# Bi-directional linear attention of a four-part vision tower: three units on VectorE become six, in two image halves

## The reference, cut to what matters

```python
# L1_attn: bi-directional linear attention over 49 tokens, then channel mixing
def _wkv_scan(w, k, v):
    ...
    def step(carry, kv):
        a, b, m = carry
        kt, vt = kv
        mm = jnp.maximum(m + w, kt)
        e1 = jnp.exp(m + w - mm)
        e2 = jnp.exp(kt - mm)
        return ((e1 * a + e2 * vt, e1 * b + e2, mm), (a, b, m))
    ...
def bi_wkv(w, u, k, v):
    ...
    kk = kt + u
    M = jnp.maximum(jnp.maximum(mf, mb), kk)
    ef = jnp.exp(mf - M)
    eb = jnp.exp(mb - M)
    ec = jnp.exp(kk - M)
    y = (ef * af + eb * ab + ec * vt) / (ef * bf + eb * bb + ec)
    ...
h = _ln(x, ln1_w, ln1_b)
k = h @ Wk_a.T
v = h @ Wv_a.T
sr = jax.nn.sigmoid(h @ Wr_a.T)
y = bi_wkv(decay / Tn, first / Tn, k, v)
x = x + sr * y @ Wo_a.T
h = _ln(x, ln2_w, ln2_b)
kf = jnp.square(jax.nn.relu(h @ Wk_f.T))
x = x + jax.nn.sigmoid(h @ Wr_f.T) * (kf @ Wv_f.T)
```

## Time and profile before

| | us |
|---|---|
| median of 3 runs | 1715.54 (1711.41 to 1716.17) |
| the profiled execution, its own time | 1713.88 |
| its span | 1712.1 |
| PE busy | 1332.6 (78%) |
| DVE busy | 985.0 (58%) |
| ACT busy | 626.3 (37%) |
| POOL busy | 550.1 (32%) |

### The profile page before, as it was taken

One profiled execution on the slowest core, in us unless ns is written; L12 is line 12 of the kernel. 1 busy time (PEld: TensorE's weight loads), 2 busy tenths in 40 slices (PEclk: granted clock), 3 DMA queues, 4 the chain that ended last, 5 costly groups with the idle time before them and its releaser, 6 DMA issues.

```text
span 1712.1 us, 18068 instructions
## 1 busy us (share of the span) xinstructions
PE 1332.6 (78%) x6516; PEld 760.3 (44%) x6516; DVE 985.0 (58%) x1582; ACT 626.3 (37%) x1114; POOL 550.1 (32%) x390
## 2 busy tenths in 40 slices
PE   6789889899898672578687745007978999989998
PEld 6444445445454341343233332003774666744444
DVE  2179999999999998730000067994253661411111
ACT  2577767767677540110000013110404224233111
POOL 0078887888878873000000010000031530100000
PEclk9789999999999987678778757555997999999999
DMA  5213142240321404037878610000012000111100
GB/s 175 85 68 123 39 143 60 92 151 15 139 89 63 150 1 171 1 140 301 336 296 322 249 49 0 0 0 0 1 28 54 1 1 1 33 58 51 33 1 29
DMA packets 41332, 151.95 MB, mean 89 GB/s; under 512 B 10364, under 2 KB 17659, under 8 KB 37020
## 3 DMA queue, kind: packets, MB, share of 16 engines
q1 hardware_dynamic: 37148, 149.21, 24.5%
q10 hardware_dynamic: 4096, 1.58, 0.4%
HBM read 147.56 MB, written 1.63 MB: 87 GB/s over the span
## 4 chain that ended last, share of the span: by engine, by line
PE 48%; DVE 20%; issue 15%; POOL 7%; DMA 6%; ACT 3%; SPq 1%; ACTq 0%; DVEq 0%; POOLq 0%
PE ps L1497 46%; DVE arena L1154 6%; DMA arena<-in_e_b 6%; POOL arena L677 4%; DVE arena L1143 4%; ACT arena L783 1%; DVE arena L1107 1%; DVE stats L1094 1%; POOL arena L698 1%; SPq L535 1%; POOL arena L686 1%; PE ps L1506 1%; POOL arena L682 1%; DVE arena L1380 1%; DMA arena<-in_patches 0%
## 5 line engine op out<-in xcount | busy, mean ns | idle before, releaser
L1497 PE MATMUL ps<-arena 128*98 128x192 f32 (+15 forms) x5200 | 975.9, 434 | 227.1 <-issue 118.9
L1497 PEld LDWEIGHTS ps<-arena 128*98 128x98 f32 (+13 forms) x5200 | 550.2, 158 | 629.9 <-issue 401.9
L677 POOL TENSOR_TENSOR arena<-arena 128x784 f32<-128x784 f32 x192 | 360.7, 1891 | 88.3 <-DVE arena L1154 87.7
L1497 PE MATMUL ps<-arena,ident 128*128 128x392 f32 x768 | 301.6, 523 | 51.0 <-POOL arena L677 50.8
L1154 DVE TENSOR_TENSOR_SCAN arena<-ps,arena 128x784 f32<-128x784 f32 x192 | 340.5, 1774 | 0.4 <-ACT ps L830 0.4
L830 ACT ACTIVATE ps<-arena 128x384 f32<-128x384 f32 x384 | 207.9, 575 | 132.9 <-DVE arena L1154 132.1
L783 ACT ACTIVATE arena<-ps 128x392 f32<-128x392 f32 (+10 forms) x261 | 115.9, 459 | 377.8 <-PE ps L1497 285.9
L1497 PEld LDWEIGHTS ps<-arena,ident 128*128 128x128 f32 x768 | 144.4, 198 | 184.5 <-POOL arena L677 91.3
L783 ACT ACTIVATE arena<-ps,arena 128x392 f32<-128x392 f32 (+2 forms) x176 | 95.3, 604 | 267.4 <-PE ps L1497 139.0
L1143 DVE TENSOR_TENSOR arena<-ps,arena 128x784 f32<-128x784 f32 x192 | 182.2, 949 | 7.7 <-ACT ps L845 7.4
L1264 DVE COPY arena<-ps 128x384 f32<-128x384 f32 x32 | 16.4, 553 | 206.2 <-PE ps L1694 206.2
(11 more groups left out here) (183 smaller groups left out, 864.8 us busy)
## 6 DMA issues: line engine op xcount, KB each, us to landing
arena<-in_e_w SPq DMA_DIRECT2D x32, 2304.0 KB
arena<-bc_rows SPq DMA_DIRECT2D x128, 392.0 KB, 4.6
arena<-in_patches SPq DMA_DIRECT2D x4, 1176.0 KB, 12.1
arena<-comb_rows SPq DMA_DIRECT2D x1, 3136.0 KB, 10.8
arena<-in_mlp_w SPq DMA_DIRECT2D x5, 576.0 KB, 6.0
arena<-arena ACTq DMA_DIRECT2D x128, 12.0 KB, 8.5
arena<-in_mlp_w SPq DMA_DIRECT2D x5, 384.0 KB, 4.9
arena<-in_mlp_w SPq DMA_DIRECT2D x10, 192.0 KB, 5.4
```

Source lines behind the costliest of these rows:

```text
L677: pool.tensor_tensor(pair(hbuf[:, at % SLOTS, :]), pair(hbuf[:, at % SLOTS, :]), c_all[:, n:n + 2, :], ALU.mult).then_inc(times_c, 1)
L1497: return pe.matmul(dst, lhsT, rhs, start=first, stop=last)
```

## The change

The linear attention is cut in six units of 392 columns (`WKV`: channels 0 to 127 of each quarter, and channels 128 to 191 of quarters 0 and 2, and 1 and 3). Each has a `front` (maximum scans and the exponents' arguments) and a `back` (the sums' scans and the products), and DVE runs front(t), back(t-1), final(t-2). Images lie with a gap column between them, 400 columns for eight images; the gap holds -1e38 or 0, so the scans reset by themselves, and the decay is added by ACT's bias. The products of numerator and denominator are summed by PE with the identity matrix (`sums`); 1/x is exp(-ln x) on ACT (`inverse`); the sigmoid is a tanh, whose 1 and 1/2 are folded into DVE's operations. Everything from W_o to the queries runs by image halves. DVE normalises only one version of each tile (`twice_normed`), ACT the other (`once`); adds go by pairs of tiles; the square is taken in place. POOL's constants and SP's loads of the weights of this part and of the next no longer wait for the mix or the channel mixing.

```diff
+WKV = ((0, 0), (0, 1), (1, 0), (1, 1), (0, 2), (0, 3))
+A_UNIT = (0, 1, 4, 5)
+B_UNIT = 2
+GAPPED = QI * (TOKENS + 1)
...
+        plan(s_kvr, 6, (0, 1, 2, 3), "act")
+        plan(s_xaT, 4, (4, 5, 6, 7), "act")
+        for t in range(7):
+            if t + 2 < 6:
+                for i in range(3):
+                    use(s_kvr, [(3 * t + i) % 2], "act")
+            if t >= 1:
+                use(s_sum, [5], "act")
+                use(s_sum, [6], "dve")
+            if t == 5:
+                plan(s_wo4, 4, (7, 0, 1, 7), "dve")
...
-            s_mix.wait_taken(sp, NT - 1)
+            s_xs.wait_taken(sp, 11)
...
-            s_vf.wait_taken(sp, NT - 1)
-            sp.wait_ge(h_plus, NT)
...
+            s_y2.wait_filled(pool, NG - 1)
+            for b in range(2):
+                own.step(pool.memset(gaps(kk[:, b, 0:GAPPED], 0), -1e38))
+                own.step(pool.memset(kk[:, b, GAPPED:GAPPED + 1], -1e38))
+            for r in range(2):
+                for v in (e1[0][r], e1[1][r], e2[0][r], e2[1][r], e2v[r]):
+                    own.step(pool.memset(gaps(v, r), 0.0))
+            own.wait()
+            pool.nop().then_inc(const_ready, 1)
+            for i in range(8):
+                s_wo4.wait_taken(pool, i)
+                pool.tensor_tensor(two_tiles(h, i), two_tiles(h, i), two_tiles(x1, i), ALU.add).then_inc(h_plus, 1)
...
-            for i in range(18):
-                which, piece, part = KVR[i]
-                dst = (kk, vv, sr)[which][:, piece * HALF + part * QT:piece * HALF + (part + 1) * QT]
-                copy_out(s_kvr, i, dst, bank(s_kvr.banks[i][0], 128, 0, QT),
-                         ACT.Sigmoid if which == 2 else ACT.Copy)
-            for p in range(3):
-                for n in range(EXPS):
-                    act.wait_ge(w_args, EXPS * p + n + 1)
-                    act.activation(ex[:, n, :], ex[:, n, :], ACT.Exp).then_inc(w_exps, 1)
...
+            def kvr_out(u):
+                if u >= 4:
+                    act.wait_ge(prod_ready, 2 * (u - 4) + 2)
+                for w, dst in enumerate((now(kk[:, u % 2, 0:GAPPED], 0), steps_of(vv[:, u % 4, :]),
+                                         steps_of(sr[:, u, :]))):
+                    i = 3 * u + w
+                    copy_out(s_kvr, i, dst, steps_of(bank(s_kvr.banks[i][0], 128, 0, QT)),
+                             *((ACT.Tanh,) if w == 2 else ()), **({"scale": 0.5} if w == 2 else {}))
+            def exps(u):
+                b, j = u % 2, WKV[u][0]
+                if u >= 2:
+                    act.wait_ge(prod_ready, 2 * (u - 2) + 2)
+                for n, r in ((0, 0), (1, 1)):
+                    act.wait_ge(w_args, 7 * u + 2 * n + 1)
+                    v = now(e1[b][r], r)
+                    act.activation(v, v, ACT.Exp, bias=wu49[:, j:j + 1]).then_inc(w_exps, 1)
+                    act.wait_ge(w_args, 7 * u + 2 * n + 2)
+                    v = now(e2[b][r], r)
+                    act.activation(v, v, ACT.Exp).then_inc(w_exps, 1)
+                for k in range(3):
+                    act.wait_ge(w_args, 7 * u + 5 + k)
+                    v = ex[b][:, k, :]
+                    act.activation(v, v, ACT.Exp, **({"bias": wu49[:, 2 + j:3 + j]} if k == 2 else {}))\
+                        .then_inc(w_exps, 1)
+            def inverse(u):
+                if u >= 2:
+                    s_sum.wait_taken(act, 2 * (u - 2) + 1)
+                copy_out(s_sum, 2 * u, rec[:, u % 2, :], bank(s_sum.banks[2 * u][0], 128, 0, QT), ACT.Ln)
+                s_sum.wait_taken(act, 2 * u)
+                act.activation(rec[:, u % 2, :], rec[:, u % 2, :], ACT.Exp, scale=-1.0).then_inc(rec_ready, 1)
+            def once(dst, i, ready, signal):
+                act.wait_ge(ready, i + 1)
+                act.activation(dst[:, i, :], h[:, i, :], ACT.Identity, bias=nmean[:, i:i + 1],
+                               scale=rs[:, 0, i:i + 1]).then_inc(signal, 1)
+            turned_in(s_xaT, range(4), 0)
+            kvr_out(0)
+            kvr_out(1)
+            turned_in(s_xaT, range(4, 8), 0)
+            for t in range(7):
+                if t < 6:
+                    exps(t)
+                if t + 2 < 6:
+                    kvr_out(t + 2)
+                if t >= 1:
+                    inverse(t - 1)
+                if t < 2:
+                    for i in range(8 * t, 8 * t + 8):
+                        once(x1, i, xa_ready, x1_once)
...
+            def front(u):
+                b, j = u % 2, WKV[u][0]
+                m_u, k_u = m_s[b], now(kk[:, b, 0:GAPPED], 0)
+                s_kvr.wait_taken(dve, 3 * u)
                 for r in range(2):
+                    dve.tensor_tensor_scan(way(m_u[r], r), way(step_w[r][j], r), way(kk[:, b, r:r + GAPPED], r),
+                                           0.0, ALU.add, ALU.max).then_inc(m_ready, 1)
+                dve.wait_ge(m_ready, 2 * u + 2)
+                own.step(TT(steps_of(top[:, b, :]), before(m_u[0], 0), before(m_u[1], 1), ALU.max))
+                for r in range(2):
+                    TT(now(e1[b][r], r), before(m_u[r], r), now(m_u[r], r), ALU.subtract).then_inc(w_args, 1)
+                    TT(now(e2[b][r], r), k_u, now(m_u[r], r), ALU.subtract).then_inc(w_args, 1)
+                own.wait()
+                own.then(STT(steps_of(top[:, b, :]), k_u, wu49[:, 2 + j:3 + j], steps_of(top[:, b, :]),
+                             ALU.add, ALU.max))
+                if u >= 2:
+                    s_sum.wait_filled(dve, 2 * (u - 2))
+                for k in range(3):
+                    TT(steps_of(ex[b][:, k, :]), before(m_u[k], k) if k < 2 else k_u, steps_of(top[:, b, :]),
+                       ALU.subtract).then_inc(w_args, 1)
+            def back(u):
+                b, v_u = u % 2, vv[:, u % 4, :]
+                dve.wait_ge(w_exps, 7 * u + 4)
+                s_kvr.wait_taken(dve, 3 * u + 1)
+                for r in range(2):
+                    own.step(TT(now(e2v[r], r), now(e2[b][r], r), steps_of(v_u), ALU.mult))
+                    own.step(dve.tensor_tensor_scan(way(b_s[r], r), way(e1[b][r], r), way(e2[b][r], r),
+                                                    0.0, ALU.mult, ALU.add))
                 own.wait()
                 for r in range(2):
+                    own.step(dve.tensor_tensor_scan(way(a_s[r], r), way(e1[b][r], r), way(e2v[r], r),
+                                                    0.0, ALU.mult, ALU.add))
+                dve.wait_ge(w_exps, 7 * u + 7)
+                if u >= 1:
+                    s_sum.wait_filled(dve, 2 * (u - 1) + 1)
+                for r in range(2):
+                    ins = TT(steps_of(prod[:, r, :]), steps_of(ex[b][:, r, :]), before(b_s[r], r), ALU.mult)
+                ins.then_inc(prod_ready, 1)
                 own.wait()
                 for r in range(2):
+                    TT(steps_of(prod[:, 2 + r, :]), steps_of(ex[b][:, r, :]), before(a_s[r], r), ALU.mult)
+                TT(prod[:, 4, :], ex[b][:, 2, :], v_u, ALU.mult).then_inc(prod_ready, 1)
+            def final(u):
+                s_kvr.wait_taken(dve, 3 * u + 2)
+                dve.wait_ge(rec_ready, u + 1)
+                if u >= 1:
+                    s_sum.wait_taken(dve, 2 * (u - 1) + 1)
+                own.then(STT(tmp, sr[:, u, :], 1.0, rec[:, u % 2, :], ALU.add, ALU.mult))
+                s_sum.wait_filled(dve, 2 * u + 1)
+                STT(sr[:, u, :], bank(s_sum.banks[2 * u + 1][0], 128, 0, QT), 0.5, tmp, ALU.mult, ALU.mult)\
+                    .then_inc(s_sum.taken["dve"], 1)
...
+            def attended(k):
+                dve.wait_ge(x1_once, 8 * k + 8)
+                for i in range(4 * k, 4 * k + 4):
+                    s_wo4.wait_filled(dve, i)
+                    TT(two_tiles(x1, i), two_tiles(x1, i), pair_of(s_wo4, i), ALU.add).then_inc(s_wo4.taken["dve"], 1)
+                norm_stats(x1, k, lambda i: s_wo4.wait_taken(dve, i // 2))
                 for i in range(8 * k, 8 * k + 8):
                     normalise(xa, x1, i, rstd).then_inc(xb_ready, 1)
...
+            def squares(k):
+                for i in range(12 * k, 12 * k + 12):
+                    q, m = divmod(i, 6)
+                    s_kf.wait_taken(dve, i)
+                    v = kf[k][:, m, q % 2 * QT:(q % 2 + 1) * QT]
+                    TT(v, v, v, ALU.mult).then_inc(kf_ready, 1)
+            def gated_sum(k):
+                for i in range(4 * k, 4 * k + 4):
+                    s_vf.wait_filled(dve, i)
+                    s_rf.wait_taken(dve, i)
+                    dve.wait_ge(h_plus, i + 1)
+                    own.then(STT(gate[:, i % 2, :], two_tiles(sig, i), 1.0, pair_of(s_vf, i), ALU.add, ALU.mult))
+                    STT(two_tiles(h, i), gate[:, i % 2, :], 0.5, two_tiles(h, i), ALU.mult, ALU.add)\
+                        .then_inc(s_vf.taken["dve"], 1)
+            for t in range(8):
+                if t < 6:
+                    front(t)
+                if 1 <= t <= 6:
```

(46 more changed lines are left out.)

481 lines of the change are left out of this document (237 added, 244 removed).

## The result

The change is faster: 1633.8 us median of four runs (1626.57 to 1641.96), beside 1713.47 us (1709.9 to 1716.17) before on the same chip; the ratio is 0.9538, with a 95% interval of 0.9484 to 0.9591. The prediction was 1631, from 1618 to 1652. The profiled execution took 1626.57 us, its span is 1624.8. One execution of the changed kernel's repeat, further down, took 6046.57 us; it is a slow run of its own kind, whose cause stays open, and all medians and ratios here are of the fast runs.

A forecast was written before the change was run, and what follows sets the result against it. Limits in turn: DVE until 1154.9, PE at low clock through W_o, then PE at high clock, with DVE's norms between. Loop load from 1322.8 to 1238.8 saves 84.0 us: 1713.9 to 1629.9, median 1631, range 1618 to 1652.

The forecast's parts named there:

- Rival B: In the units, ScalarE's sums, table loads, logarithm and exponential end on the path: 34 us, 1665; chance 0.04.
- the sums' 44.1, 21.3 and 26.2: PE's pieces after turns, from receptance 5.5, hidden layer 15.8, W_o's second half 7.1, output 15.7, queries and keys 10.5.
- rival C: The halves don't hide the norms; two norms and a start-up stand in PE's way: 20 us, 1651; chance 0.07.
- section 3: PE from last numerator to loop: 117.4 us plus 3.3 for the clock; norms lie under outputs and first queries.
- So 0 to 6.9 us; I take 2: Before the mix: SP's earlier loads beside ScalarE's last copies of expert rows cost 2 us.
- No wait in the units: DVE sets the pace at the high clock, units every 15.0 us with no wait on ScalarE.
- Rival A: PE stays at the low clock through the units: 18 us, 1649; chance 0.10.
- the 16 that the prediction gave as a sign of being wrong: In DVE's units: the forecast is wrong if units come further apart than 16 us.
- W_o at a mixture of clocks: W_o's first half takes 14.2 us at low clock, 7.1 at high; 4 us of waiting and adds taken.
- The distance to the end unchanged: The loop's first DVE product comes near 1241 and its distance to the end stays unchanged.
- turns 3.1: PE between last numerator and loop: turns counted three times at 3.1 us each.
- The signs that name a time from the span's start (1017, 1022, 1118, 1241): DVE's first scan near 1017, wrong if later than 1022; PE's last numerator near 1118; loop's first product near 1241.

The follow-up runs named there:

- the changed kernel's repeat: The changed kernel run again unaltered: 1635.55 us, ratio 0.9537 to the kernel before.
- e2: Changed kernel with the reciprocal alone back on VectorE, ScalarE only copying the denominator out of PSUM: 1652.94 us.
- e6: Changed kernel with the first half's queries and keys moved behind the turns of the second half: 1643.57 us.
- e1: Changed kernel with SP's early loads issued only once all of the experts' rows are in place: 1634.05 us, ratio 0.9525.
- e10: Changed kernel loading early only k, v, r weights and small vectors; other early loads await the experts' rows, PE awaits W_o's weights at W_o alone: 1627.45 us.
- e9: Changed kernel with ScalarE writing its version of the mix's tiles in units 3 and 4 instead of 0 and 1: 1631.68 us.
- e8: Changed kernel with VectorE writing both versions of each normalised tile and ScalarE neither: 1638.35 us, ratio 0.9577.
- e7: Changed kernel with unread products added on PE behind the sums of units 1 to 3 and before unit 5's numerator: 1631.22 us.
- e3: Changed kernel with the sums of numerator and denominator back on VectorE, PE bringing each to PSUM by one identity product: 1643.68 us.
- e4: Changed kernel with the numerators alternating between two PSUM banks, 6 and 4: 1627.34 us, ratio 0.9489.
- e11: Changed kernel with split loads, late ScalarE version, GpSimd behind the last norm, two numerator banks, W_o's first pairs early with an own bank for the last: 1620.2 us.

## Why the prediction was right

The path of the forecast held: DVE's units, then the last numerator behind final(4), then PE's row of work to the loop, with the norms under it. The closeness of the sum is in part luck, as the second list shows.

**What was right by its own steps.** The first scan stands 22.8 us behind the mix (22.6 and hops). Scans of 400 columns take 0.98 to 0.99 us, strided views cost nothing, a unit is 14.48 where 15.0 was said (*final* 1.08 instead of 1.2, with a PSUM operand at 567 ns, and a little of front and back each). The units' end is 88.0 us behind the first scan, 87.6 said, and that agreement is luck: without its two waits, 3.4 us, the stretch is 84.6, 3.0 under the forecast, and the two errors cancel. Rival B's price is zero: e2 shows that ScalarE's work with its twelve table loads is under DVE's. The Trainium skill, ScalarE: Activation LUTs, What ACT_TABLE_LOAD costs, adds a drain to each load. In this trace no drain shows: the load of 1.28 us at 1063.82 is followed by its instruction at 1065.12, and VectorE has no wait on ScalarE in the units. PE got its last numerator 14.2 us behind the units' end (13.1 said), and the pieces from there, 44.78, 21.24 and 26.33 us, are the sums' 44.1, 21.3 and 26.2. No rival C: e6 prices the norm that is hidden at 9 us, in the cover that section 3 named.

**What was not.** Five terms. The copies, the waits and the distance to the end cost; W_o's clock was wrong without a gain; the last gave back.

- *"So 0 to 6.9 us; I take 2"* for the row copies. It was 5.9 (7.5 against 1.6), and e1 and e10 bring it back to 1.5. The reason given, that most bytes are through by 990, did not help: what counts is that the copies of 976.37 to 981.37 land late, 7.3 us after their issue where e10 has 2.0. The loads also began earlier than said, at 961.7 instead of 971.
- *No wait in the units.* Rival A came true in part: 1.62 and 1.77 us in the fronts, and 2 us for the numerator. With these waits the fronts came 16.07 and 16.21 us apart twice, over the 16 that the prediction gave as a sign of being wrong; the unit's own length, 14.48, was not what was wrong, but the wait that it took to be nothing. I had put it down to the low clock; e9 and e8 show that it was ScalarE's other version of the norm's tiles, which the prediction counted as hidden (8.6 us of 15 and 3.4 to 4 more) without asking what stands behind them in that queue. e7, at a higher clock, leaves the pace of the later units as it was, but its added work stands behind both waits.
- *W_o at a mixture of clocks.* It ran at the high clock, 7.93 us, straight behind the sums; 7.1 was said for that clock. The rule that I had weighed against it, that activity releases the throttle (the Trainium skill, TensorE: Matmul & The Clock Gate, Part 1), fits this trace. It doesn't fit e3, where PE is busy with W_o for 14.00 of 14.00 us at 0.50, as before. The 3 us that I gave the rule did not come: W_o begins only at 1096.57, 3.2 us before the units' end, and DVE's additions go at its pace (waits of 0.27, 1.43 and 1.43 us). Wait and additions took 5.3 us for the 4 that I took.
- *The distance to the end unchanged.* It is 391.4 instead of 387.4, 4.0 worse, and in eight of the twelve other profiles too it is 391.2 to 391.4 (389.9 to 394.5 in the rest); of the kernel before there is one profile. The part of it that is found, 3.2 us, is the clock's in the MLPs (last section).
- *Three times "turns 3.1".* That row was at the low clock; here they take 1.82, 1.51 and 1.51. That gave back some 4 us. The low clock on the numerator (4.26 for 2.0) and in the queries cost about the 3.3 that were added for it. Numerator to loop took 117.5 us instead of 120.7, the numerator came 1.1 later than said, and 2.1 are left from the units' end to the loop.

The upstream stretch, 9.4 us shorter in this one profile, made the profiled time (1626.57) better than the forecast for it (1629.9); the median of 1633.8 lies 2.8 above the forecast for a median. With the stretches as measured, of which the upstream one is left out, the sum is 84.0 - 3.9 (copies) + 0.3 (scan) - 0.4 (units) + 2.1 (units' end to loop) - 4.0 (behind it) = 78.1; the measured medians are 79.7 apart, and the 1.6 between them is within their spread. The forecast said 84.0: the misses, 8.3 us, were larger than the 2.4 that came back. That 1631 comes within 2.8 of 1633.8 owes 2.1 us to the kernel before, whose median was 1715.54 when the forecast was made and is 1713.47 now. The signs that name a time from the span's start (1017, 1022, 1118, 1241) move with the upstream stretch: the first scan stands at 1011.70 here and at 1024.87 in the repeat.

## What to carry to other kernels

Where one engine works alone, cut its work into staggered units and give what others can do under its cover away; the price is then counted on the engine that sets the pace (2.6 us for a reciprocal of 392 columns, 0.48 for a product). What such a count misses stands in queues: a bank that two items in a row share (e4), a side job ahead of a result (e9), a load moved into the traffic that it was kept behind (e1, e10). A load put off again pays only if no wait bundles it with one that is needed sooner.

## What the runs showed of the hardware

The clock gave part of two gains back. Where the wait ahead of the turns was shortened, the hole that stayed had a slow stretch behind it (e4: 2.9 us of 7.8; e11: 4.6 of 9.9). And the same hole does not always cost the same. PE in order of time in the changed kernel's MLPs:

```profile
1390.33 13.12 PE L1641 MATMUL ps<-arena 128*128 128x392 f32 x48 [1.59 <-ACT arena L844]
...
1407.27 17.94 PE L1641 MATMUL ps<-arena 128*4 128x392 f32 x48 [2.33 <-ACT arena L844]
```

and at the same place in the kernel before, which runs the same instructions there:

```profile
1481.51 14.81 PE L1497 MATMUL ps<-arena 128*128 128x392 f32 x48 [1.59 <-ACT arena L783]
...
1500.14 14.77 PE L1497 MATMUL ps<-arena 128*4 128x392 f32 x48 [2.33 <-ACT arena L783]
```

The waits are alike to 0.01 us, but here the clock fell behind the second, there behind the first: 3.2 us more for one, 1.7 less for the other. With 6.08 against 4.39 us for the next products of 392 columns that is 3.2 of the 4.0 us; why it falls where it does stays open.

W_o's products ran for 7.92 us at 1.00 in e4, and for 28.28 us before and 14.00 us in e3 at 0.50 throughout, while receptance behind it in e3 ran at 1.00. The mix's products, which print the same form, ran while the clock rose: 0.50 from 988 to 992 us and 0.96 from 992 to 996 in the changed kernel. What sets W_o apart stays open.

Small operations of VectorE took three and a half times as long (0.60 instead of 0.17 us) beside GpSimd's tensor products; its normalisations of 192 columns took 0.48 instead of 0.30 us each. The Trainium skill, SBUF — State Buffer, SBUF: two separate sides, says that a GpSimd operation and a VectorE operation in a two-port mode, or with two inputs in SBUF while GpSimd reads SBUF, take a shared pair of ports as an exclusive lock for a whole instruction. The trace agrees: GpSimd's products take 0.65 us each (5.20 for 8), and VectorE's root operations come at that pace.
